# Splitting a per-head norm pass into eight parts and moving the softmax epilogue two iterations forward in an attention and FFN layer

## What is computed

```python
q = jnp.concatenate([q_c, q_r], axis=-1)                      # 64 + 32 wide
k = jnp.concatenate([k_c, jnp.broadcast_to(k_r, ...)], axis=-1)
scale = 1.0 / (H ** 0.5 + ROPE_HEAD_DIM ** 0.5)
scores = jnp.einsum('bhqd,bhkd->bhqk', q, k) * scale
attn = jax.nn.softmax(scores, axis=-1)
out = jnp.einsum('bhqk,bhkd->bhqd', attn, v)
```

## Time and profile before

| | us |
|---|---|
| median of 2 runs (10,722.96 and 10,929.83) | 10,826.39 |
| profiled execution, slowest core | 10,671.3 |
| its span (core 5) | 10,669.8 |
| spans of the 8 cores | 10,595.3 to 10,669.8 |
| TensorE busy | 7,722.2 (72%) |
| ScalarE busy | 3,481.7 (33%) |
| VectorE busy | 3,354.0 (31%) |

### The profile page before, as it was taken

How to read it: one execution, slowest core, us unless ns; L and a number is a source line. 1 busy time by engine, 2 the same in 40 slices (tenths; PEclk the granted TensorE clock), 3 DMA queues, 4 the chain that set the end, 5 groups by cost and what they waited for, 6 DMA issues and landing times.

```text
span 10669.8 us, 93799 instructions; the slowest of 8 cores (10595.3 to 10669.8 us)
## 1 busy us (share of the span) xinstructions
PE 7722.2 (72%) x33278; PEld 3203.0 (30%) x33278; DVE 3354.0 (31%) x3792; ACT 3481.7 (33%) x4205; POOL 3.5 (0%) x15
## 2 busy tenths in 40 slices
PE   3555668888878888554332159999999997879976
PEld 1211212222222222122221124444444443334432
DVE  3333323222232222477785320000000016620023
ACT  1222247777767777322332110000000002320011
POOL 0000000000000000000000000000000000000000
PEclk9777768888888888766555579999999997779987
DMA  2111110000000000222575443333333334456599
GB/s 94 65 57 41 49 60 12 6 12 6 12 6 12 6 6 6 85 111 115 187 270 187 130 123 107 107 112 114 107 107 107 107 95 162 154 178 200 173 281 311
DMA packets 400422, 1089.87 MB, mean 102 GB/s; under 512 B 28258, under 2 KB 257634, under 8 KB 337507
## 3 DMA queue, kind: packets, MB, share of 16 engines
q1 hardware_dynamic: 399972, 1083.88, 31.5%
HBM read 771.19 MB, written 312.61 MB: 102 GB/s over the span
## 4 chain that ended last, share of the span: by engine, by line
PE 58%; DVE 20%; DMA 12%; ACT 5%; issue 4%; DVEq 0%; SPq 0%; ACTq 0%
PE ps_g L1273 11%; PE ps_u L1283 11%; PE ps_s L765 9%; PE ps_av L742 9%; PE ps_dB L1556 7%; DVE rvb_sb L799 4%; PE ps_d L1416 4%; DMA hqT_sb<-hqT_hbm 3%; DMA w2raw<-w_down 2%; PE ps_c L411 2%; DVE qmD L1081 2%; DVE statC L892 1%; DVE tmp L668 1%; ACT x_sb L916 1%; DMA xq_sb<-xq_hbm 1%
## 5 line engine op out<-in xcount | busy, mean ns | idle before, releaser
L788 ACT ACTIVATE probs<-ps_s,negc_bc 128x1024 bf16<-128x1024 f32 x2048 | 2092.1, 1143 | 684.9 <-PE ps_s L765 682.8
L765 PE MATMUL ps_s<-qh_sb,kh_sb 96*128 96x512 bf16 x4096 | 1317.8, 410 | 98.1 <-ACT probs L788 90.4
L1273 PE MATMUL ps_g<-w1g,xq_sb 128*128 128x512 bf16 x5632 | 1293.0, 384 | 124.8 <-DMA xq_sb<-xq_hbm 124.8
L1283 PE MATMUL ps_u<-w1u,xq_sb 128*128 128x512 bf16 x5632 | 1273.3, 380 | 0.0
L742 PE MATMUL ps_av<-probs,v_sb 128*65 128x512 bf16 x4096 | 1242.7, 399 | 32.0 <-DVE ao_sb L824 32.0
L1556 PE MATMUL ps_dB<-w2b,hqT_sb 128*128 128x512 bf16 x4224 | 976.5, 396 | 152.8 <-DMA hqT_sb<-hqT_hbm 142.4
L799 DVE RECIPROCAL rvb_sb<-ps_av 1x1024 bf16<-1x1024 f32 x64 | 419.3, 6552 | 1888.0 <-PE ps_av L742 1830.7
L1306 DVE TENSOR_TENSOR hst<-sg_sb,ps_u 128x512 bf16<-128x512 f32 x352 | 242.2, 688 | 2344.0 <-PE ps_u L1283 2271.7
L1299 ACT ACTIVATE sg_sb<-ps_g 128x512 f32<-128x512 f32 x352 | 210.1, 597 | 2319.8 <-PE ps_g L1273 2286.9
L1273 PEld LDWEIGHTS ps_g<-w1g,xq_sb 128*128 128x128 bf16 x5632 | 554.7, 99 | 807.0 <-issue 156.0
L1283 PEld LDWEIGHTS ps_u<-w1u,xq_sb 128*128 128x128 bf16 x5632 | 550.6, 98 | 664.9
(11 more groups left out here) (140 smaller groups left out, 5573.8 us busy)
## 6 DMA issues: line engine op xcount, KB each, us to landing
xq_sb<-xq_hbm SPq DMA_DIRECT2D x352, 512.0 KB, 3.7
hqT_sb<-hqT_hbm SPq DMA_DIRECT2D x96, 1408.0 KB, 8.3
w1raw<-w_gate_up SPq DMA_DIRECT2D x22, 4096.0 KB, 19.5
w1qT_hbm<-stg SPq DMA_DIRECT2D x22, 2048.0 KB, 8.3
w2raw<-w_down SPq DMA_DIRECT2D x8, 5632.0 KB, 30.2
h_hbm<-hst SPq DMA_DIRECT2D x352, 128.0 KB, 3.2
h_sb<-h_hbm SPq DMA_DIRECT2D x32, 1408.0 KB, 7.8
hqT_hbm<-hqstg SPq DMA_DIRECT2D x32, 1408.0 KB, 6.2
```

Of the source, the lines that this page charges most:

```text
L765: h.matmul(ps_s[sb2][:, 512 * j:512 * (j + 1)], kh_sb[:, buf * L + 128 * c: buf * L + 128 * (c + 1)], qh_sb[:, buf * L + q0 + 512 * j: buf ...
L788: "scalar", lambda h, pb=pb, hd=hd, sb2=sb2: h.activation(probs[:, pb * QBL:(pb + 1) * QBL], ps_s[sb2][:, :], AF.Exp, bias=negc_bc[:, hd:h ...
L1273: h.matmul(ps_g[pg][:, :], xq_sb[:, tb * D + 128 * dc: tb * D + 128 * (dc + 1)], w1g[:, buf * DC * 512 + dc * 512: buf * DC * 512 + (dc + ...
L1283: h.matmul(ps_u[pg][:, :], xq_sb[:, tb * D + 128 * dc: tb * D + 128 * (dc + 1)], w1u[:, buf * DC * 512 + dc * 512: buf * DC * 512 + (dc + ...
```

## The change

Two edits. The epilogue of a block goes into the streams behind score pair 1 of the next block, in place of score pair 3. And `head_norm1` is cut into `L // 512` = 8 parts of two matmuls with their reductions; in the loop they stand, at `qb == 1`, behind the AV pair of the iterations `c` = 5, 8, 11, ... 26, in place of one run at `c == 4`. The waits within the norm are the same, with the marks of the reductions kept between the parts in `norm_red`. The first head still runs all parts in a row, ahead of the loop.

```diff
@@ -646,16 +646,19 @@
                                 ALU.mult), dve)
         sq_pool_mk = dve.val
 
-    def head_norm1(hd):
+    norm_red = {}
+
+    def head_norm1_part(hd, part):
         nonlocal ps_rb_free, sq_rd
-        k.wait("tensor", dve, max(sq_mk))
-        k.wmark("tensor", ps_rb_free)
-        red_mk = {}
         NJ = L // 512
-        for idx in range(2 * NJ):
+        if part == 0:
+            k.wait("tensor", dve, max(sq_mk))
+            k.wmark("tensor", ps_rb_free)
+            norm_red.clear()
+        for idx in (2 * part, 2 * part + 1):
             which, j = idx // NJ, idx % NJ
             if idx >= 2:
-                k.wait("tensor", dve, red_mk[idx - 2])
+                k.wait("tensor", dve, norm_red[idx - 2])
             nm = k.emit("tensor", lambda h, idx=idx, which=which, j=j:
                         h.matmul(
                             ps_rb[0:16, 512 * (idx % 2):512 * (idx % 2) + 512],
@@ -665,7 +668,7 @@
                             start=True, stop=True), pe)
             k.wait("vector", pe, nm)
             k.wait("vector", dve)
-            red_mk[idx] = k.emit("vector", lambda h, idx=idx: h.reduce_max(
+            norm_red[idx] = k.emit("vector", lambda h, idx=idx: h.reduce_max(
                 tmp16[:, :],
                 ps_rb[0:16, 512 * (idx % 2):512 * (idx % 2) + 512],
                 axis=AX.X), dve)
@@ -677,11 +680,16 @@
                 k.emit("vector", lambda h, which=which: h.tensor_tensor(
                     qn_h[:, which:which + 1], qn_h[:, which:which + 1],
                     tmp16[:, :], ALU.max), dve)
-        sq_rd = pe.val
-        k.wait("vector", dve)
-        k.emit("vector", lambda h: h.tensor_tensor(
-            tmp16[:, :], qn_h[:, 0:1], qn_h[:, 1:2], ALU.mult), dve)
-        ps_rb_free = (dve, dve.val)
+        if 2 * part + 1 == 2 * NJ - 1:
+            sq_rd = pe.val
+            k.wait("vector", dve)
+            k.emit("vector", lambda h: h.tensor_tensor(
+                tmp16[:, :], qn_h[:, 0:1], qn_h[:, 1:2], ALU.mult), dve)
+            ps_rb_free = (dve, dve.val)
+
+    def head_norm1(hd):
+        for p in range(L // 512):
+            head_norm1_part(hd, p)
 
     def head_norm2(hd):
         nonlocal ps_rb_free
@@ -769,15 +777,16 @@
                                           buf * L + q0 + 512 * (j + 1)],
                                     start=True, stop=True), pe)
                 sc_mk = pe.val
-                if c == min(3, KC - 1) and pending_epi is not None:
+                if c == min(1, KC - 1) and pending_epi is not None:
                     pending_epi()
                     pending_epi = None
                 if c >= 5:
                     emit_av(c - 5)
                 if hd + 1 < NH and QB > 1 and c == 6 and qb == 0:
                     head_sq(hd + 1)
-                if hd + 1 < NH and QB > 1 and c == 4 and qb == 1:
-                    head_norm1(hd + 1)
+                if (hd + 1 < NH and QB > 1 and qb == 1 and c >= 5
+                        and (c - 5) % 3 == 0 and (c - 5) // 3 < L // 512):
+                    head_norm1_part(hd + 1, (c - 5) // 3)
                 if hd + 1 < NH and QB > 1 and c == 4 and qb == 2:
                     head_norm2(hd + 1)
                 k.wait("scalar", dve, negc_hd_mk)
```

## The result

The changed kernel is faster: the ratio of its runs to those of before is 0.9857, 95% interval 0.9828 to 0.9886, that is 1.4%, about 150 us of 10,700. Its 11 runs took 10,538 to 11,315 us with a median of 10,768.8, and the 10 runs of before, beside it, 10,693 to 11,463 with a median of 11,112.3. The medians scatter so widely because in many executions, of every kernel, the matmuls of some cores run slower from some point on (in one such stretch 512 columns took 0.26 us instead of 0.22); the ratio leaves those runs out, and so do the times of runs given with the experiments and the cores on which lengths are read. The profiled execution took 10,610.5 us; core 5 is shown, as before.

The account below looks back on a forecast made before the run. ScalarE's exponentials were taken to set the pace, leaving idle time at block ends to win. A norm gain of 203 us less a boundary loss of 38, rounded to 160, off 10,775 gave 10,615 us; range 10,465 to 10,770.

Parts of the forecast that it names:

- -165: Whole change, all in the attention phase: 203 us gained on the norm less 38 us lost at boundaries.
- within 2%: Outcome class for the whole kernel, taken as not told from no change (2%, 216 us); chance 0.83.
- the base: Whole kernel's time before, 10,775 us, the mean of three times, from which 160 us was taken.
- Part 1: Epilogue moved from c == 3 to c == 1: 0.6 us lost at each of 63 boundaries, 38 us, bounds 0 and 145.
- should come back no later: TensorE's clock at a plain boundary: shorter gaps after 6.70 us bring it back no later, so the loss is 0.6 us.
- Part 2: head_norm1 in eight parts: its cost per head falls from 16.0 to 2.5 us, 203 us gained over 15 heads.
- the 2.5 us left over: Norm block of each head: norm cost still showing after the cut into parts, 2.5 us, bounds 0.9 to 3.9.
- Slack of 3 x 0.14 = 0.43 per part: TensorE in the norm block: slack of three iterations, 0.43 us, set against each part's two matmuls of 0.22 us.
- short, and I leave them out: The 16 extra weight loads of the norm parts, 88 ns each, counted as nothing; 21 us worse if not hidden.
- B: Rival: boundaries lose nothing and only the first norm part shows, 226 us gained, 10,549 us; chance 0.12.
- C: Rival: the clock stays low through the norm block, 223 us slower in all, 10,998 us; chance 0.05.
- D: Rival: boundary and norm costs both at upper bounds, low clock longer, only 37 us gained, 10,738 us; chance 0.15.

Follow-up runs that it names:

- kernel with the epilogue alone: Against the kernel before, only the epilogue moved to c == 1, head_norm1 still in one run at c == 4; attention phase 2,930.1 us, times 10,715.5 to 10,767.7 us.
- parts alone: Against the kernel before, only head_norm1 cut into parts, the epilogue still at c == 3; attention phase 2,686.3 us, times 10,527.9 and 10,534.5 us.
- the kernel with the useless matmuls: Changed kernel plus 26 matmuls without use on TensorE ahead of the wait for the reciprocal; attention phase 2,676.9 us, whole time 10,517.7 us.
- the kernel with the tail moved: Against the kernel that copies ps_av first, the last five AV pairs go into the next block; attention phase 2,224.5 us, whole time 10,063.3 us.

## Why the prediction was right and wrong

**Which steps failed.** The two mechanisms were right, a loss at each boundary and a large gain in the norm block, but both terms of the sum were mis-sized in the same direction. The boundary was put at 0.6 us and measured 0.9, because the clock did come back later in some blocks. What is left of the norm was put at 2.5 us a head and measured 3.7, because slack was added up over three iterations and the weight loads were put at nothing. In the attention phase -165 became -127.

**The total.** -160 us, 1.5%, was forecast; the ratio says 1.4%. That they agree so well is in part luck: the attention phase gained 127 us, and the interval of the ratio (122 to 184 us) holds that and the forecast alike. Wrong, besides the two terms, is the step from the sum to the chances. "A measurement of this kernel tells about 2% from no change" was taken from the spread of two runs, and 0.83 went to "within 2%" on a forecast of a clear 1.5%. Four runs of the changed kernel lie within 0.3% (10,538 to 10,574; the profiled one, 10,610.5, is 0.7% above the lowest), the interval is 0.3% to either side, and the change stands well clear of none.

**The absolute time.** 10,615 was forecast and the median is 10,768.8, 1.4% above the forecast and 1 us inside the range (10,465 to 10,770), which is luck: neither has to do with the change. The step that failed is the base, the mean of three times, 10,775, of which one, 10,929.8, lies 2.4% above the lowest. Later, before's own median was 11,112.3. A median here depends on how many of the executions had slower matmuls. Only the ratio was predictable.

**Part 1, +38 forecast, +56 measured.** The sequence at the boundary, worked out for exponentials 2 to 6 as 8.79, 9.79, 11.18, 12.18 and 13.88, was met to two hundredths in the medians of core 5 (8.79, 9.80, 11.16, 12.17, 13.87). It gave 0.9 us of loss with the clock back at 14.4. The kernel with the epilogue alone shows 0.9 per boundary too, but as a mean of unlike blocks, so that agreement is luck: 0.7 in the fourth blocks of a head, where the clock came back as before; 1.5 in the first and 1.2 in the norm blocks; 0.2 in head_norm2's, where 0.45 was forecast. The mistake is the choice of 0.6 on the argument that the clock "should come back no later". It came back at 16.4 in the block shown, and exponential 7 started at 15.58 instead of 15.1.

**Part 2, -203 forecast, -188 measured** (parts alone). That the long run's 16 us would become a few was right, and so was that no norm matmul would wait for a reduction: in the loop no matmul of line 663 has idle time ahead of it put down to VectorE. The term that failed is the 2.5 us left over: it measured 16.0 - 12.3 = 3.7, near the upper bound of 3.9; seven parts at 0.44 make 3.1 of it. "Slack of 3 x 0.14 = 0.43 per part" added up slack over iterations that can only be used in one, and the extra weight loads, "short, and I leave them out", cost 0.20 us a part (0.10 before and after) though their busy time is 0.09. The sentence on the Trainium skill there ("TensorE: Matmul & The Clock Gate", "Step-by-step: what each phase is for") was held to agree with loads pulled ahead. For the AV and score pairs it does; for the 96x16 weights between them this case shows the load right at the matmul, and for 96x128 weights the load 0.21 us ahead.

**The rivals.** B (all hides) and C (the clock stays low in the norm block) did not come. The clock of the norm block is 0.89 after, 0.76 before. D named the right reason for the shortfall of part 1, the longer low clock, at too high a price; the shortfall of part 2 no rival named. The same page's section "Why this matters for your kernels" warns of idle gaps between bursts of matmuls; I had argued that a clock already lost can't be lost again. The traces say otherwise for some blocks: with the gap grown from 3.49 to 6.01 us it was low for 13.7 us instead of 10.2 in 11 of 31 plain blocks, and for 10.2 as before in the other 20, which had the same gap. So the longer gap makes the longer low clock possible but doesn't decide it. What does is open, since also in the kernel with the useless matmuls it fell in some blocks and not in others of the same make.

## What to carry to other kernels

Where two engines hand work to each other over two buffers, write down the loop time: slack of the engine that isn't the bound could not be saved up over three iterations here, so inserted work belongs in small single pieces, spread evenly (one matmul in every second iteration cost 0.05 us for eight, one in every iteration 0.08 us each). A consumer moved ahead in an in-order queue brings its wait with it, and everything behind pays; it is better to free what is waited for (here a 1.2 us copy ahead of a 6.55 us reciprocal, with the epilogue after it, took the changed kernel's attention phase from 2,747 to 2,318 us) than to move the wait. And count low clock as a cost of its own behind every wait (here 2.3 to 2.7 us per boundary), and compare blocks with an equal length of low clock before you judge a gain of 1 us.

## What the runs showed of the hardware that was not expected

Between matmuls with weights of 96x128 or 128x65 a pair starts 0.43 us after the last; with weights of 96x16 in between, 0.53 us, both going to them and coming back. With the same ones widened to 96x128 it is 0.43 again. Fewer columns of weights made the matmul no cheaper and its neighbours dearer. The two broadcast matmuls of the epilogue, with weights of 1x64, are no cheaper for their neighbours either: in the kernel with the tail moved they start 0.52 us behind a score pair, and the AV pair 0.55 behind them. Which shapes belong to the dear kind was not tried further.
